# Moving the split of x ahead of the softmax's two stages, and the low parts of N to one engine

## The chip, the cores and the metric

The kernel runs on one core of a Trainium2 chip. The metric is the device time of one execution in microseconds (us). A core has TensorE (PE in the profile, its weight loads PEld), VectorE (DVE), ScalarE (ACT), GpSimd (POOL) and SyncE (SP), which here only issues DMAs. Each engine works through its own instructions in order; semaphores join them.

## The reference

Sixteen batches of 1024 rows of width 512. Each row of x attends to the 64 context rows of its batch with 16 heads of width 64, the result is added to x, and a chain of three 512x512 matrices with a tanh is added to that. Cut to its core:

```python
def xattn(x, latents, shift, scale, ...):      # x: context (64 rows a batch), latents: layernorm(x), 1024 rows
    xn = layernorm(x, ln1_w, ln1_b); ln = layernorm(latents, ln2_w, ln2_b)
    q = ln @ Wq; k, v = split(xn @ Wkv)
    q = q * (1 + scale) + shift                # by batch and head
    attn = softmax(einsum('bihd,bjhd->bhij', q, k) / 8)
    return einsum('bhij,bjhd->bihd', attn, v) @ Wout
x = x + xattn(ctx_1024, layernorm(x), fside, fside, ...)
x = x + tanh(layernorm(x) @ weight @ aux_weight1 @ aux_weight2 + bias)
```

## The kernel before, in words

The work is folded so that a tile of 128 rows needs few matmuls. For each batch, Wq and k are multiplied ahead into one matrix M (512 x 1024: 16 heads times 64 context rows), v and Wout into one matrix N (1024 x 512), and the three feed-forward matrices into W3. Every fp32 operand of a matmul is split in two fp32r parts, a high one (a cast on ScalarE, written `..._hi`) and a low one (the rest, by a subtraction on VectorE or GpSimd, `..._lo`), and a product is three passes: high by high, high by low, low by high (`passes`, line 162; line 168 issues the passes that need the high part of the tile, line 173 those that need its low part).

There are T = 128 tiles, 8 to a batch. `run` calls one function for each engine and slot t (`slot_pe`, `slot_act`, `slot_dve`, `slot_pool`, `slot_sp`), and the order of the calls in each function is the order of that engine's queue, written out by hand. It is a pipeline over slots. In slot t:

- PE makes the scores of tile t in two halves q = 0 and 1 of 512 columns (24 matmuls, from `xT_hi` and `xT_lo`, which are single buffers), then the output product of tile t-2 in two halves (24 matmuls, from `pT_hi`, `pT_lo` and N), then the feed-forward product of tile t-4 (12 matmuls). Between them stand matmuls for the M and N of later batches: four short ones (lines 937 to 940) up to slot 89, and four (lines 756, 757) in the slots that make N.
- DVE: turning and low part of the second half of p of tile t-2, then for each half the scale and bias of the scores (line 1399) and the row maximum (1404), then for each half the sum (1410) and its reciprocal (1413), then the addition of the output to x (1511), then the turning (1421) and low part (1430) of the first half of p of tile t-1.
- POOL: the last addition of tile t-5 (1571), then the subtraction of the maximum (1547) for both halves, with the low part of a landed piece of M between them (1021), then the two normalisations (1554), then `xT_lo` of tile t+1 (1085) and two small powers (1070, 1559).
- ACT: `pT_hi` of the second half (1296), the tanh (1337), the statistics of the second layernorm, `x2T_hi`, the high part of a piece of M (1017), the first exponential (1291), the statistics of the first layernorm of tile t+1 (1052 to 1059), the second exponential, `xT_hi` of tile t+1 (1080), evacuations, and `pT_hi` of the first half of tile t-1.
- SP issues all DMAs in one queue: the turned x of tile t+1 at the slot's start (`load_xT`, line 639, which waits for `xT_lo` of tile t), x of tile t+2, four reads of p that turn it between partitions (1145), four of x2 (1157), the result (1166), pieces of M, and, behind the normalisations, the two writes of p (1127).

From batch 4 on N is made in pairs of batches. In each of the 8 slots t = 8(b-1)+2+p PE makes two banks for the head pair p of batches b and b+1 (`n2_pe`), ACT evacuates bank 0 and DVE bank 1 (`n2_evacuate`, two copies of 64 partitions each, lines 765 and 766) to a raw buffer. The split into `N_hi` (`n2_hi`, line 775, ACT) and `N_lo` (`n2_lo`, line 781) of the even batch comes in one go at the **border slot** t = 33, 49, 65, 81, 97 and 113 (`border(t)`: the second slot of an even batch from 4 on), since the buffers come free only there: eight pieces. ACT makes pieces 0 to 3, then `pT_hi`, then 4 to 7. DVE makes the low parts of pieces 0 and 1 ahead of `pT_lo`, and of 2, 3 and 7 behind it; POOL makes 4, 5 and 6. The odd batch has one piece a slot, on DVE. PE waits for the low parts through `n2_made` in the slot after.

```python
BY_POOL = (4, 5, 6)
border = lambda t: t % TPB == 1 and t // TPB in range(STACKED, B, 2)
def xT_split_hi(act, u):            # also waits for the scores of tile u - 1: xT_hi is a single buffer
    act.wait_ge(s_xT, 16 * u if u else 16)
    at_least(act, s_sc[1], u)
```

## Time and profile before

| what | value |
|---|---|
| median of 3 runs | 2071.06 us (2065.18 to 2071.54) |
| profiled execution, its own time | 2069.4 us |
| its span | 2067.6 us |
| granted TensorE clock, mean over the span | 0.997 |
| PE, PEld busy | 2017.8 us (98%), 1661.6 us (80%) |
| DVE, ACT, POOL busy | 1573.8 us (76%), 1364.1 us (66%), 1393.7 us (67%) |
| DMA packets' time, share of 16 engines, queue of SP | 79.2% |

The profile is one execution. The span runs from its first instruction to its last, 1.8 us short of the execution's own time. Matmuls are pipelined: in a full PE one of 512 columns starts every 0.227 us and each is shown as 0.39 us long, so the idle time ahead of a matmul in the rows is less than what its start is late. In the chain of work that ended last PE has 32%, DVE 18%, SP's queue 15%, ACT 10%.

### The profile page before, as it was taken

What the parts mean: (1) busy time and instruction counts of PE and PEld (TensorE: products, weight loads), DVE (VectorE), ACT (ScalarE), POOL (GpSimd) and SP (SyncE); (2) the same over time, 40 slices, a digit from 0 to 9 for tenths busy, and PEclk for the clock granted to TensorE, in tenths of its full rate; (3) what the DMA queues carried; (4) which work ended last, traced back from release to release, by engine and by line L of the source; (5) the groups of instructions that cost most, each with busy time, mean ns of one, the idle gap of its engine ahead of it and who ended that gap; (6) DMA issues with size and microseconds to landing.
All of it is one profiled execution on the core that took longest, in us unless ns stands there. A gap on an engine that the chain in (4) does not pass through costs nothing.

```text
span 2067.6 us, 31929 instructions
## 1 busy us (share of the span) xinstructions
PE 2017.8 (98%) x9072; PEld 1661.6 (80%) x9072; DVE 1573.8 (76%) x2470; ACT 1364.1 (66%) x3125; POOL 1393.7 (67%) x1529
## 2 busy tenths in 40 slices
PE   8998999999999999999999999999999999999998
PEld 6887878888788788878888788878888788878887
DVE  7567876776677787787777877778777877888776
ACT  4455667666676766776667676666666666666654
POOL 2136767666577777677766777777776777777664
PEclk9999999999999999999999999999999999999999
DMA  7657989989788788978898798888877567866663
GB/s 259 196 176 219 275 233 256 265 241 262 210 249 256 207 236 242 260 217 225 233 260 242 205 234 238 243 229 221 230 228 241 171 204 208 236 197 196 189 171 121
DMA packets 524864, 464.11 MB, mean 224 GB/s; under 512 B 56720, under 2 KB 416272, under 8 KB 524688
## 3 DMA queue, kind: packets, MB, share of 16 engines
q1 hardware_dynamic: 524688, 462.06, 79.2%
q8 instruction: 74, 1.21, 0.3%
q14 instruction: 102, 0.84, 0.1%
HBM read 279.64 MB, written 182.26 MB: 223 GB/s over the span
## 4 chain that ended last, share of the span: by engine, by line
PE 32%; DVE 18%; SPq 15%; ACT 10%; issue 10%; POOL 7%; DMA 4%; DVEq 0%; ACTq 0%; POOLq 0%
PE bank L168 12%; PE bank L1246 8%; PE bank L173 6%; POOL area L1547 5%; PE bank L1251 4%; DVE pT_lo L1430 3%; ACT area L1291 3%; DVE turned L1421 3%; DVE area L1399 2%; ACT pT_hi L1296 2%; DVE row_max L1404 2%; SPq L1127 2%; SPq L726 2%; SPq L1145 2%; SPq L1157 2%
## 5 line engine op out<-in xcount | busy, mean ns | idle before, releaser
L1547 POOL TENSOR_TENSOR area<-area,row_max 128x256 f32<-128x256 f32 x512 | 353.0, 710 | 105.3 <-DVE row_max L1404 100.1
L1296 ACT CAST pT_hi<-turned 128x512 fp32r<-128x512 f32 x256 | 159.3, 622 | 400.8 <-DVE turned L1421 400.7
L168 PE MATMUL bank<-M_hi,xT_hi 128*128 128x512 f32 x1024 | 402.7, 393 | 14.4 <-ACT xT_hi L1080 14.4
L168 PE MATMUL bank<-M_lo,xT_hi 128*128 128x512 f32 x1024 | 401.4, 392 | 0.0
L1571 POOL TENSOR_TENSOR area<-area 128x512 f32<-128x512 f32 x127 | 165.4, 1302 | 269.1 <-ACT area L1337 269.1
L1554 POOL TENSOR_TENSOR area<-area,row_inv 128x512 f32<-128x512 f32 x256 | 269.1, 1051 | 113.7 <-DVE row_inv L1413 113.7
L1410 DVE TENSOR_REDUCE row_sum<-area 128x8 f32<-128x512 f32 x256 | 174.5, 682 | 169.5 <-ACT area L1291 168.6
L1430 DVE TENSOR_TENSOR pT_lo<-turned,pT_hi 128x512 fp32r<-128x512 f32 x256 | 196.6, 768 | 112.3 <-ACT pT_hi L1296 103.7
L173 PE MATMUL bank<-M_hi,xT_lo 128*128 128x512 f32 x1024 | 276.0, 391 | 3.6 <-POOL xT_lo L1085 3.6
L1246 PE MATMUL bank<-N_hi,pT_hi 128*128 128x512 f32 x640 | 249.5, 390 | 3.2 <-ACT pT_hi L1296 1.8
L1246 PE MATMUL bank<-N_lo,pT_hi 128*128 128x512 f32 x640 | 249.6, 390 | 1.5 <-issue 1.4
L168 PEld LDWEIGHTS bank<-M_hi,xT_hi 128*128 128x128 f32 x1024 | 193.8, 189 | 57.5 <-ACT xT_hi L1080 17.3
L1291 ACT ACTIVATE area<-area 128x512 f32<-128x512 f32 x256 | 160.4, 626 | 115.6 <-POOL area L1547 115.5
L173 PEld LDWEIGHTS bank<-M_hi,xT_lo 128*128 128x128 f32 x1024 | 190.9, 188 | 48.6 <-POOL xT_lo L1085 9.8
L168 PEld LDWEIGHTS bank<-M_lo,xT_hi 128*128 128x128 f32 x1024 | 194.0, 189 | 39.8
L168 PE MATMUL bank<-W_hi,x2T_hi 128*128 128x512 f32 (+1 forms) x512 | 199.1, 389 | 1.1 <-ACT x2T_hi L1317 1.1
L168 PE MATMUL bank<-W_lo,x2T_hi 128*128 128x512 f32 (+1 forms) x512 | 199.1, 389 | 0.0
L1399 DVE SCALAR_TENSOR_TENSOR area<-bank,rs,area 128x512 f32<-128x512 f32 x256 | 185.6, 725 | 3.4 <-DMA m_scratch<-area 3.4
L1421 DVE STREAM_TRANSPOSE turned<-p_moved 128x512 f32<-128x512 f32 x256 | 180.5, 705 | 5.3 <-DMA p_moved<-p_scratch 1.4
L1404 DVE TENSOR_REDUCE row_max<-area 128x8 f32<-128x512 f32 x256 | 175.7, 686 | 8.8
L1056 ACT ACTIVATE bank<-area,st 128x512 f32<-128x512 f32 x254 | 175.9, 693 | 8.3
L1450 DVE TENSOR_TENSOR x2T_lo<-turned,x2T_hi 128x512 fp32r<-128x512 f32 x126 | 109.3, 868 | 86.6 <-ACT x2T_hi L1317 85.4
(211 smaller groups left out, 4547.9 us busy)
## 6 DMA issues: line engine op xcount, KB each, us to landing
p_scratch<-area SPq DMA_DIRECT2D x256, 256.0 KB, 3.1
p_moved<-p_scratch SPq DMA_DIRECT2D x512, 128.0 KB, 4.2
area<-x_dram SPq DMA_DIRECT2D x128, 256.0 KB, 5.0
area<-x_turned_dram SPq DMA_DIRECT2D x128, 256.0 KB, 4.4
x_scratch<-area SPq DMA_DIRECT2D x127, 256.0 KB, 3.4
x_moved<-x_scratch SPq DMA_DIRECT2D x508, 64.0 KB, 3.5
y_dram<-area SPq DMA_DIRECT2D x127, 256.0 KB, 3.5
land<-m_scratch SPq DMA_DIRECT2D x120, 256.0 KB, 3.2
```

Source lines behind the costliest of these rows:

```text
L168: mm = eng.matmul(ps, sh, mv, start=(n == 0), stop=False)
L173: mm = eng.matmul(ps, sl, mh, start=False, stop=(k == len(pairs) - 1))
L1056: act.activation(junk_ps[:], src, ACT.Square, bias=st[:, 1:2], accum_out=st[:, 2:3]).then_inc(s_sq, 1)
L1246: mm = pe.matmul(O_ps[:], st(pT_hi, k), n_cols(mv, k), start=(k == 0 and mv is hi), stop=False)
L1291: act.activation(s, s, ACT.Exp).then_inc(s_ex[q], 1)
L1296: act.copy(half_of(pT_hi, q), turned[:]).then_inc(s_pTh[q], 1)
L1399: dve.scalar_tensor_tensor(out=half_of(S[t % 2], q), in0=S_ps[q][:], scalar=rs1[:, 0:1], in1=half_of(bias, q), op0=ALU.mult, op1=ALU.add). ...
L1404: dve.tensor_reduce(row_max[t % 2][:, q * H2:(q + 1) * H2], heads(half_of(S[t % 2], q)), AX_XY, ALU.max).then_inc(s_mx[q], 1)
L1421: dve.transpose(turned[:].rearrange("p (k g r) -> p k g r", k=4, g=4), blocks).then_inc(done, 1)
L1430: dve.tensor_tensor(half_of(pT_lo, q), turned[:], half_of(pT_hi, q).bitcast(F32), ALU.subtract).then_inc(s_pTl[q], 1)
L1547: last = pool.tensor_tensor(s, s, row.to_broadcast([P, 2, 4, J2]), ALU.subtract)
L1554: pool.tensor_tensor(s, s, inv, ALU.mult).then_inc(s_p[q], 1)
```

## The change

In every slot t from 3 on, ACT makes `xT_hi` of tile t+1 ahead of the first exponential instead of behind the second, and POOL makes `xT_lo` of tile t+1 ahead of the two normalisations instead of behind them. At the border slots DVE makes all eight low parts, in two groups of 2 and 6, and ACT evacuates both banks. The counters of the semaphores follow.

```diff
--- before.py
+++ after.py
@@ -603,7 +603,7 @@
         s_n, s_nh, s_nl = sem("s_n"), sem("s_nh"), sem("s_nl")
         s_bin = sem("s_bin")
         s_x2a, s_x2n = sem("s_x2a"), sem("s_x2n")
-        s_last, s_nfree, s_nl_pool = sem("s_last"), sem("s_nfree"), sem("s_nl_pool")
+        s_last, s_nfree = sem("s_last"), sem("s_nfree")
         s_yl, s_bnl, s_rsl = sem("s_yl"), sem("s_bnl"), sem("s_rsl")
         s_kh, s_kl = sem("s_kh"), sem("s_kl")
         s_wo2, s_nev = sem("s_wo2"), sem("s_nev")
@@ -696,9 +696,6 @@
             used, free = free[1], (used, free[0])
         N_of = lambda b: [n_bufs[i] for i in n_at[b]]
         stage_of = lambda b, c: n_raw[:, (n_at[b][1] * PAIRS + c) * D:(n_at[b][1] * PAIRS + c + 1) * D]
-        BY_POOL = (4, 5, 6)
-        BY_DVE = {0: [c for c in range(PAIRS) if c not in BY_POOL], 1: list(range(PAIRS))}
-        lo_before = lambda b: PAIRS * min(b, STACKED) + sum(len(BY_DVE[a % 2]) for a in range(STACKED, b))
         split_at = {TPB * b + c - TPB + 2: (b, c) for b in range(STACKED + 1, B, 2) for c in range(PAIRS)}
         border = lambda t: t % TPB == 1 and t // TPB in range(STACKED, B, 2)
         n2_ps = banks[2:4]
@@ -778,14 +775,7 @@
             for c in cs:
                 eng.wait_ge(s_nh, PAIRS * b + c + 1)
                 hi, lo = (n_cols(y, c) for y in N_of(b))
-                eng.tensor_tensor(lo, stage_of(b, c), hi.bitcast(F32),
-                                  ALU.subtract).then_inc(s_nl if c in BY_DVE[b % 2] else s_nl_pool, 1)
-
-        def n2_made(pe, b, q):
-            of_half = range(4 * q, 4 * q + 4)
-            pe.wait_ge(s_nl, lo_before(b) + sum(c < 4 * q + 4 for c in BY_DVE[b % 2]))
-            if b % 2 == 0 and any(c in BY_POOL for c in of_half):
-                pe.wait_ge(s_nl_pool, len(BY_POOL) * ((b - STACKED) // 2) + sum(c < 4 * q + 4 for c in BY_POOL))
+                eng.tensor_tensor(lo, stage_of(b, c), hi.bitcast(F32), ALU.subtract).then_inc(s_nl, 1)
 
         m_where = lambda c: ((c // 2) % 4, 2 * (c // 8) + c % 2)
         in_pairs = lambda a: a.rearrange("p (i a j) -> p i a j", i=2, j=J2)
@@ -1234,10 +1224,8 @@
                 at_least(pe, s_x2, u)
             for q in range(2):
                 if tile_of(t - 2):
-                    if m == 2 and u < TPB * STACKED:
+                    if m == 2:
                         pe.wait_ge(s_nl, u + 4 + 4 * q)
-                    elif m == 2:
-                        n2_made(pe, u // TPB, q)
                     hi, lo = N_of(u // TPB)
                     ks = range(4 * q, 4 * q + 4)
                     pe.wait_ge(s_pTh[q], u + 1)
@@ -1349,6 +1337,8 @@
                 xT_split_hi(act, t + 1)
             if t > 2:
                 evacuate("A")
+                if t < T - 1:
+                    xT_split_hi(act, t + 1)
             if t < T:
                 exp(0)
             if t < 2:
@@ -1365,12 +1355,13 @@
                 fold_n_act(act, 0, range(5, 6))
                 land_hi(act, 0)
                 fold_n_act(act, 0, range(6, 7))
-            elif t < T - 1:
+            elif t == 2:
                 xT_split_hi(act, t + 1)
-            if t == 2:
                 ln1_stats(act, 3, 3)
             if t in stacked_at:
                 n2_evacuate(act, act.copy, *stacked_at[t], 0)
+                if border(t):
+                    n2_evacuate(act, act.copy, *stacked_at[t], 1)
             evacuate("C")
             if border(t):
                 n2_hi(act, t // TPB, range(0, 4))
@@ -1511,7 +1502,8 @@
                 dve.tensor_tensor(xr[u % RING], O_ps[:], xr[u % RING], ALU.add).then_inc(s_x2, 1)
             sum_tile("C")
             if t in stacked_at:
-                n2_evacuate(dve, dve.tensor_copy, *stacked_at[t], 1)
+                if not border(t):
+                    n2_evacuate(dve, dve.tensor_copy, *stacked_at[t], 1)
             if tile_of(t - 1):
                 if t >= 4:
                     dve.wait_ge(s_x2Tl, t - 3)
@@ -1523,13 +1515,13 @@
                     maximum(0, 2)
                 turn_p(0, t - 1)
                 if border(t):
-                    n2_lo(dve, t // TPB, BY_DVE[0][0:2])
+                    n2_lo(dve, t // TPB, range(0, 2))
                 if t == 1:
                     read_scores(1, 2)
                     maximum(1, 2)
                 pT_lo_part(0, t - 1)
             if border(t):
-                n2_lo(dve, t // TPB, BY_DVE[0][2:])
+                n2_lo(dve, t // TPB, range(2, 8))
             if t in split_at:
                 b, c = split_at[t]
                 n2_lo(dve, b, [c])
@@ -1590,19 +1582,17 @@
             if t == 2:
                 land_lo(pool, 1)
                 xT_split_lo(pool, 3)
+            if 2 < t < T - 1:
+                xT_split_lo(pool, t + 1)
             if t < T:
                 normalise(0)
                 normalise(1)
             if t == 1:
                 land_lo(pool, 0)
-            if 2 < t < T - 1:
-                xT_split_lo(pool, t + 1)
             if 1 < t < T - 1:
                 pow1(pool, t + 1)
             if tile_of(t - 4) and t - 4 < LAST - 1:
                 pow2(t - 4)
-            if border(t):
-                n2_lo(pool, t // TPB, BY_POOL)
             if t == 5:
                 land_lo(pool, t)
```

The border slot t = 33 on ACT. In this listing an instruction's line is that of its own file; `Wo_hi<-n_raw,N_lo` and `N_lo<-n_raw` name the buffers that hold N at that batch. Before:

```order
L1017 CAST M_hi<-land 128x512
L1291 ACTIVATE area<-area 128x512
L1052 ACTIVATE bank,st<-area 128x512
L1054 ACTIVATE st<-st 128x1
L1056 ACTIVATE bank,st<-area,st 128x512
L1059 ACTIVATE var<-st,eps 128x1
L1291 ACTIVATE area<-area 128x512
L1080 CAST xT_hi<-area 128x512
L765 COPY n_raw<-bank 64x512
L766 COPY n_raw<-bank 64x512
L968 COPY evac<-bank 128x2x4x64
L775 CAST N_lo<-n_raw 128x512 x4
```

and now:

```order
L1007 CAST M_hi<-land 128x512
L1070 CAST xT_hi<-area 128x512
L1279 ACTIVATE area<-area 128x512
L1042 ACTIVATE bank,st<-area 128x512
L1044 ACTIVATE st<-st 128x1
L1046 ACTIVATE bank,st<-area,st 128x512
L1049 ACTIVATE var<-st,eps 128x1
L1279 ACTIVATE area<-area 128x512
L762 COPY n_raw<-bank 64x512
L763 COPY n_raw<-bank 64x512
L762 COPY n_raw<-bank 64x512
L763 COPY n_raw<-bank 64x512
```

The cast of `xT_hi` stands ahead of the first exponential (the first ACTIVATE of area), and a second pair of copies has come in ahead of the casts of N.

The same slot on POOL, before:

```order
L1021 TENSOR_TENSOR M_lo<-land,M_hi 128x512
L1547 TENSOR_TENSOR area<-area,row_max 128x256 x2
L1554 TENSOR_TENSOR area<-area,row_inv 128x512 x2
L1085 TENSOR_TENSOR xT_lo<-area,xT_hi 128x512
L1070 TENSOR_TENSOR rs<-var,minus_half 128x1
L1559 TENSOR_TENSOR rs<-var,minus_half 128x1
L781 TENSOR_TENSOR Wo_hi<-n_raw,N_lo 128x512 x3
```

and now:

```order
L1011 TENSOR_TENSOR M_lo<-land,M_hi 128x512
L1539 TENSOR_TENSOR area<-area,row_max 128x256 x2
L1075 TENSOR_TENSOR xT_lo<-area,xT_hi 128x512
L1546 TENSOR_TENSOR area<-area,row_inv 128x512 x2
L1060 TENSOR_TENSOR rs<-var,minus_half 128x1
L1551 TENSOR_TENSOR rs<-var,minus_half 128x1
```

`xT_lo` has gone ahead of the normalisations (two instructions on row_inv), which it does in the other slots too, and the three low parts of N are gone. On DVE, behind the addition to x, before:

```order
L1511 TENSOR_TENSOR area<-bank,area 128x512
L765 COPY n_raw<-bank 64x512
L766 COPY n_raw<-bank 64x512
L1421 STREAM_TRANSPOSE turned<-p_moved 128x512
L781 TENSOR_TENSOR Wo_hi<-n_raw,N_lo 128x512 x2
L1430 TENSOR_TENSOR pT_lo<-turned,pT_hi 128x512
L781 TENSOR_TENSOR Wo_hi<-n_raw,N_lo 128x512 x3
```

and now:

```order
L1502 TENSOR_TENSOR area<-bank,area 128x512
L1412 STREAM_TRANSPOSE turned<-p_moved 128x512
L778 TENSOR_TENSOR Wo_hi<-n_raw,N_lo 128x512 x2
L1421 TENSOR_TENSOR pT_lo<-turned,pT_hi 128x512
L778 TENSOR_TENSOR Wo_hi<-n_raw,N_lo 128x512 x6
```

The two copies have left DVE, and the last group of low parts has grown from three to six.

## Rows read from the trace of the kernel before

**Rows 1.** The page, part 1: busy time, share of the span, instructions
```profile
PE 2017.8 (98%) x9072; PEld 1661.6 (80%) x9072; DVE 1573.8 (76%) x2470; ACT 1364.1 (66%) x3125; POOL 1393.7 (67%) x1529
```

**Rows 2.** Waits of PE: waiter and its line <- whom it waited for, us in total, times, longest
```profile
PE bank L168 <- ACT xT_hi L1080: 14.4, 7, 2.5
...
PE bank L173 <- POOL xT_lo L1085: 3.6, 6, 0.8
```

**Rows 3.** Timeline, PE: start us, us long; first matmuls of slots 34, 35, 36, 38
```profile
664.52 0.39 PE L168 MATMUL bank<-M_hi,xT_hi 128*128 128x512 f32 x1
...
681.83 0.79 PE L168 MATMUL bank<-M_hi,xT_hi 128*128 128x512 f32 x1 [2.09 <-ACT xT_hi L1080]
...
697.62 0.39 PE L168 MATMUL bank<-M_hi,xT_hi 128*128 128x512 f32 x1
...
725.82 0.39 PE L168 MATMUL bank<-M_hi,xT_hi 128*128 128x512 f32 x1
```

**Rows 4.** Timeline, slot 34: POOL's first normalisation and xT_lo; ACT's xT_hi
```profile
680.42 1.05 POOL L1554 TENSOR_TENSOR area<-area,row_inv 128x512 f32<-128x512 f32 x1
...
683.36 1.29 POOL L1085 TENSOR_TENSOR xT_lo<-area,xT_hi 128x512 fp32r<-128x512 f32 x1
...
681.17 0.60 ACT L1080 CAST xT_hi<-area 128x512 fp32r<-128x512 f32 x1
```

**Rows 5.** Timeline, border slot 33: low parts of N on DVE and on POOL
```profile
666.87 5.18 DVE L781 TENSOR_TENSOR Wo_hi<-n_raw,N_lo 128x512 fp32r<-128x512 f32 x3
...
666.76 4.74 POOL L781 TENSOR_TENSOR Wo_hi<-n_raw,N_lo 128x512 fp32r<-128x512 f32 x3 [0.83 <-ACT N_lo L775]
```

**Rows 6.** Lines 781, 765, 1430: duration ns min/median/max, first and last start us
```profile
L781 DVE TENSOR_TENSOR Wo_lo<-n_raw,N_hi x16: 679/680/686, 685.1 to 1495.3; 128x512 fp32r<-128x512 f32 x16
...
L765 ACT COPY n_raw<-bank x48: 572/577/583, 558.2 to 1839.7; 64x512 f32<-64x512 f32 x48
...
L1430 DVE TENSOR_TENSOR pT_lo<-turned,pT_hi x256: 681/693/1025, 174.3 to 2049.7; 128x512 fp32r<-128x512 f32 x128
```

**Rows 7.** Line 639, the load of the turned x: all 128; that of slot 65
```profile
DMA to landing us min/median/max: 2.9/4.4/6.8
...
area<-x_turned_dram SPq DMA_DIRECT2D x1, 256.0 KB, 5.7
```

**Rows 8.** Timeline, SP: that load's issue in border slots 33, 65, 81, 97
```profile
655.06 0.84 SPq L639 DMA_DIRECT2D area<-x_turned_dram  x1
...
1129.06 0.71 SPq L639 DMA_DIRECT2D area<-x_turned_dram  x1
...
1369.05 0.75 SPq L639 DMA_DIRECT2D area<-x_turned_dram  x1
...
1597.87 0.47 SPq L639 DMA_DIRECT2D area<-x_turned_dram  x1
```

**Rows 9.** Timeline, ACT: the first exponential of the same slots
```profile
658.17 0.63 ACT L1291 ACTIVATE area<-area 128x512 f32<-128x512 f32 x1 [0.82 <-POOL area L1547]
...
1131.88 0.63 ACT L1291 ACTIVATE area<-area 128x512 f32<-128x512 f32 x1 [0.71 <-POOL area L1547]
...
1371.86 0.63 ACT L1291 ACTIVATE area<-area 128x512 f32<-128x512 f32 x1 [0.71 <-POOL area L1547]
...
1604.38 0.64 ACT L1291 ACTIVATE area<-area 128x512 f32<-128x512 f32 x1 [0.82 <-POOL area L1547]
```

**Rows 10.** Timeline, DVE: the scores' scaling, first half, in slots 100 and 101
```profile
1648.83 0.71 DVE L1399 SCALAR_TENSOR_TENSOR area<-bank,rs,area 128x512 f32<-128x512 f32 x1
...
1662.60 0.71 DVE L1399 SCALAR_TENSOR_TENSOR area<-bank,rs,area 128x512 f32<-128x512 f32 x1
```

**Rows 11.** Timeline, slot 103: pT_lo on DVE beside xT_lo on POOL
```profile
1685.71 0.96 DVE L1430 TENSOR_TENSOR pT_lo<-turned,pT_hi 128x512 fp32r<-128x512 f32 x1 [0.81 <-ACT pT_hi L1296]
...
1684.82 1.30 POOL L1085 TENSOR_TENSOR xT_lo<-area,xT_hi 128x512 fp32r<-128x512 f32 x1
```

**Rows 12.** Timeline, slot 33: POOL's second normalisation
```profile
662.44 1.05 POOL L1554 TENSOR_TENSOR area<-area,row_inv 128x512 f32<-128x512 f32 x1 [0.89 <-DVE row_inv L1413]
```

## The prediction

> **What bounds the kernel now.** I read the page's busy shares first. PE has 98% [rows 1], so nearly all of the span is matmul work that this change leaves alone; what can be gained is the time in which PE stands still. The table of PE's waits comes next: of the waits on another engine in the tile loop the largest is for `xT_hi` of the next tile, 14.4 us in 7 waits, with 3.6 us for `xT_lo` behind it [rows 2]. So I looked for the place. The starts of the slots' first matmuls give it [rows 3]: slots 36 and 37 together take 725.82 - 697.62 = 28.20 us, 14.10 each, and slots 34 and 35, with the same matmuls, take 697.62 - 664.52 = 33.10. So 4.9 us are lost behind the border slot 33, and 2.09 of them show as PE idle until ACT has cast `xT_hi` [rows 3]. A border comes six times; with one such wait from the last unstacked fold these are the 7 waits. All borders together are worth about 6 x 4.9 = 29 us.
>
> Why is ACT late there? Because the ring of the softmax is: ACT, DVE and POOL hand a tile round (scaling, maximum, subtraction, exponential, sum, normalisation, turning, split), and a border adds eight casts and eight low parts. In ordinary slots the ring needs 13.77 us: that is the distance of the first scaling of slot 100 to that of slot 101 [rows 10], while PE's own work there is 60 matmuls, at the 0.227 us of a full PE 13.6 us (the 14.10 of [rows 3] has four short ones more). Up to slot 97 PE has slots of 14.1 us and more, so the ring catches up between borders. Behind slot 97 it hardly can.
>
> **Part 1: `xT_lo` and `xT_hi` go forward.** `xT_lo` starts at 683.36 in slot 34, and the first normalisation, whose place it takes, at 680.42: it comes 2.94 us earlier [rows 4]. Its own 1.29 us now stand ahead of both normalisations. The second waits for its sums anyway, idle for 0.89 us in slot 33 [rows 12], so I charge it 1.3 - 0.9 = 0.4 us, the first 1.3; the two writes of p on SP's queue stand behind them, with the second write's followers (x2's write, loads of weights, the next turned x). Cover: p is read a slot later. `xT_hi`'s 0.60 us [rows 4] go into ACT's idle 0.82 or 0.71 us ahead of the first exponential, where it waits for POOL [rows 9]: no cost if x has landed, and 0.6 us less behind the second exponential. PE's wait is then for `xT_lo`, so I take 2.94 us a border.
>
> **Part 2: the border's low parts.** Three of them on DVE take 5.18 us while POOL's three take 4.74 in the same microseconds [rows 5]; on DVE alone one is 0.68 [rows 6]. So the two engines hold each other up, 1.73 us each instead of 0.68. Now DVE's group is six: 6 x 0.68 = 4.1 instead of 5.18, 1.1 us less. The Trainium skill, SBUF — State Buffer, section Who interferes with whom, has DVE instructions with two SBUF inputs and GpSimd's reads exclude each other for a whole instruction; these rows agree. A price without that rule, DVE at its present 1.73 for each of six, would be 10.4 us and a border 5.2 us longer. Against the 1.1 stands the second evacuation: two copies at 0.58 [rows 6] on ACT ahead of the casts of N, less the `xT_hi` that left, 1.16 - 0.60 = 0.6 us later. Bounds 0.5 and 1.1; I take **0.8 us**, since DVE in turn loses its own two copies ahead of the first low part.
>
> **Part 3: the added wait.** ACT's queue now stops ahead of the first exponential until the turned x has landed, and everything of the softmax stands behind it. The load is issued in the same slot, by SP, at the tail of its queue, and lands 2.9 to 6.8 us later, 4.4 in the median [rows 7]. With 0.7 us for the cast and its start, the exponential can begin, against its start now [rows 8, 9]:
> slot 33: 655.06 + 4.4 + 0.7 = 660.2, 2.0 us later than 658.17;
> slot 49: taken as 1.0, between slot 33's 2.0 and slot 97's nothing;
> slot 65: landing 5.7 here [rows 7], 1129.06 + 6.4 = 1135.5, 3.6 us later than 1131.88;
> slot 81: 1369.05 + 5.1 = 1374.2, 2.3 us later than 1371.86;
> slot 97: 1597.87 + 5.1 = 1603.0, ahead of 1604.38: nothing. Slot 113 I take as slot 97.
> This delay goes round the ring into the border and comes off the gain.
>
> **The sum.** A stall can be given back once, since the ring is caught up before the next border:
> border 33: 2.94 + 0.8 - 2.0 = 1.7;
> border 49: 2.94 + 0.8 - 1.0 = 2.7;
> border 65: 2.94 + 0.8 - 3.6 = 0.1;
> border 81: 2.94 + 0.8 - 2.3 = 1.4.
> Behind slot 97 the ring sets the end (13.77 against 13.6), and there the 2.94 only let PE run ahead of work it must wait for at the end. What counts is what the ring itself loses: 2 x 0.8 = 1.6 us, and in the slots where `xT_lo` on POOL overlaps `pT_lo` on DVE 0.96 [rows 11] - 0.69 [rows 6] = 0.27 us, in about 20 slots 5.4 us, since the new place has only reductions of one input beside it. Of these 7.0 I take 5.0, as PE's own 13.6 caps the ring at 0.17 a slot wherever no stall is left to give back. Sum 1.7 + 2.7 + 0.1 + 1.4 + 5.0 = **10.9 us**. The profiled execution had 2069.4 us, 1.7 under the median of the runs; 2069.4 - 10.9 = 2058.5, and I forecast **2058.5 us** as the median.
>
> **The rivals.**
> *A: every border stall goes.* The load lands in time because SP's queue, too, follows the ring, and PE finds no second thing late. 29 us less: **2040 us**. Against it: rows 8 and 9, and that `pT_hi` of the first half is the next thing PE needs, with slack of the same size as the gain. Chance 0.10.
> *B: nothing moves.* The late load of part 3 takes back what part 1 gives, in the last stretch too (0 to 4 us gained): **2068 us**. For it: in slot 65 it does so to 0.1 us, and SP's queue gets its writes of p 0.4 to 1.3 us later, which makes the load later still. PE's 98% speak for it in a general way. The Trainium skill, Perfetto Trace Analysis, section Identifying the Most-Contended Engine, has one speed up the engine with the highest occupancy and not judge TensorE by its matmul busy time; PE's matmuls lose nothing here, so by the first half of that rule the gain is nil, and rows 3 show where the busy share hides 4.9 us. Chance 0.25.
> *C: slower.* The wait closes a ring that was open: load of the turned x, `xT_hi`, exponentials, second normalisation, second write of p, and behind it on SP the next such load. Worked out: landing 4.4, cast and start 0.7, start of the first exponential to end of the second normalisation 662.44 + 1.05 - 658.17 = 5.3 [rows 9, 12] plus the 0.4 of part 1, write to next load 2.6 (an estimate: four issues of 0.5 to 0.8 as in [rows 8]), together 13.4 us. It decides once the landing averages over 4.6 us in slots where PE has 13.6 (over 5.1 where it has 14.1). At a mean landing of 5.2 us, still well inside 2.9 to 6.8, it is 14.2 us: 0.6 over in some 22 slots, 0.1 over in some 24, +15.6 us, less the 5.9 that borders 33 to 81 give: 2069.4 + 9.7, **2079 us**. Against it: the median of 4.4. Chance 0.10.
> My forecast has the remaining 0.55.
>
> **How the numbers follow.** About 0.3%, 6.2 us, is what a measurement of this kernel can tell from no change. Faster by more than that: nearly all of the forecast, whose lower end (0.5 a border at part 2, 2 us for the last stretch) is a gain of 5.9 - 1.2 + 2 = 6.7, and A; where the loads are later than I put them it falls under 6.2, so 0.62. Within 0.3%: B and that part, 0.28. Slower: C, 0.10. The range: A's 2040 and C's 2079 are left out with 0.2 between them; from the forecast with the last stretch at its full 7.0 us, the load never late (+8.9, of which border 49 can't use all) and part 2 at 1.1 a border, I get a gain of about 21, 2048; B's upper end with the median's own scatter is 2070. So 2048 to 2070.
>
> **What would show it.** In the profile after, PE's wait for ACT `xT_hi` should be almost gone behind the borders, with PE waiting for `xT_lo` or `pT` instead. The low parts of N on DVE should last 0.68 us each and none be on POOL. ACT should show idle time ahead of `xT_hi` whose releaser is the DMA from the turned x, longest around slot 65. `pT_lo` should be at 0.69 in all ordinary slots. Slots 34 and 35 should take about 1.7 us less than 33.1. I am wrong if ACT does not wait for the load at the borders (then A), or if the first scalings in slots 100 to 106 are not nearer than 13.77 us (then B), or farther (then C).

## The result

The changed kernel takes 2079.49 us (median of 5 runs, 2077.00 to 2083.62), the kernel before in the same comparison 2068.09 (5 runs, 2065.18 to 2071.54): ratio 1.0055, interval 1.0035 to 1.0075. It is slower by more than the 0.3% that can be told from no change. The prediction was 2058.5 us and faster. The profiled execution of the changed kernel had 2077.0 us, a span of 2075.2.

Part 1 of the page of the changed kernel (compare [rows 1]), then three rows of the kernel before and of the changed kernel each, from the view that cuts the span into stretches. The stretches end at the first scores matmul of slots 10, 26 and 36 and at the span's end. Columns: stretch, its length, busy us of each engine with the number of instructions, mean granted clock of TensorE, share of the DMA engines, GB/s.

```profile
PE 2017.7 (97%) x9072; PEld 1664.3 (80%) x9072; DVE 1539.9 (74%) x2476; ACT 1365.6 (66%) x3137; POOL 1323.8 (64%) x1511
```
Kernel before:
```profile
292.09:540.23 248.14, 245.93 (x1139) 203.81 (x1138) 176.88 (x278) 168.38 (x381) 168.15 (x184) 1.00 0.90 244
540.23:697.62 157.39, 151.85 (x675) 124.01 (x673) 117.74 (x183) 107.27 (x248) 109.87 (x122) 0.99 0.83 238
697.62:2067.60 1369.98, 1347.76 (x6009) 1110.63 (x6007) 1067.35 (x1651) 917.77 (x2132) 986.10 (x1081) 1.00 0.78 218
```
Changed kernel:
```profile
293.39:559.35 265.96, 249.42 (x1138) 204.95 (x1137) 170.60 (x278) 165.30 (x381) 161.73 (x184) 0.99 0.83 228
559.35:719.24 159.89, 152.20 (x674) 123.80 (x673) 114.60 (x181) 107.91 (x249) 102.81 (x118) 0.99 0.82 232
719.24:2075.20 1355.96, 1342.87 (x6009) 1110.89 (x6007) 1043.43 (x1660) 921.48 (x2142) 931.29 (x1067) 1.00 0.80 221
```

The last stretch gained 14.0 us, and for it the prediction had 9.2. Slots 26 to 36, with the first border, lost 2.5 where 1.7 were to be gained. Slots 10 to 26, of which the prediction does not speak, lost 17.8 us: more than the whole loss of the span, 7.6 (the first 10 slots and the set-up are 1.3 us longer, the rest of that difference). DVE, ACT and POOL are less busy there than before, and PE's 3.5 us more come with a clock of 0.99 instead of 1.00; nobody has more work in these slots, somebody waits. Each stretch is one execution, and that of the changed kernel was 2.5 us under its median. From slot 26 on the run "split early from slot 26" below has the changed kernel's code, and its profile has 4.7 us more there (1520.6 against 1515.9). So the 17.8 us stand clear of such scatter, the 2.5 do not by themselves. The table of waits says who waits (changed kernel; waiter and line <- whom it waited for, us in total, times, longest):

```profile
ACT evac L958 <- DMA m_scratch<-evac: 51.2, 18, 4.3
ACT xT_hi L1070 <- DMA area<-x_turned_dram: 34.4, 33, 2.7
PE bank L929 <- ACT evac L958: 11.5, 8, 1.7
PE bank L1234 <- ACT pT_hi L1284: 8.1, 6, 1.9
PE bank L753 <- issue: 6.5, 6, 2.1
PE bank L173 <- POOL xT_lo L1075: 1.0, 4, 0.4
```
PE's wait for `xT_hi` [rows 2] has left the table, as forecast. In its place PE waits for an evacuation at line 958, and ACT waits there for a DMA. The same wait in the kernel before:
```profile
ACT evac L968 <- DMA m_scratch<-evac: 24.7, 17, 4.1
```

**The ring that was not seen.** In slots 10 to 25 PE makes two short tiles a slot for the M of later batches, at two places in its queue that the code calls C and D. Both leave through one buffer, `evac` (`evacuate` and `store` in the slot functions). ACT copies C into it behind the second exponential; SP stores it, behind the second write of p, the write of x2 and a load; when the store has landed, ACT copies D, near the head of its queue for the next slot, and the exponentials stand behind that. That closes a ring: each of these steps waits for the one before, once round in every slot. One round in the kernel before (ACT, then SP; start us, length, engine and line, what, idle time before it and what ended that):

```profile
354.82 0.59 ACT L968 COPY evac<-bank 128x512 f32<-128x512 f32 x1 [1.33 <-DMA m_scratch<-evac]
...
361.36 0.63 ACT L1291 ACTIVATE area<-area 128x512 f32<-128x512 f32 x1 [0.32 <-POOL area L1547]
...
362.40 0.58 ACT L968 COPY evac<-bank 128x512 f32<-128x512 f32 x1
...
369.92 0.59 ACT L968 COPY evac<-bank 128x512 f32<-128x512 f32 x1 [1.53 <-DMA m_scratch<-evac]
...
364.15 0.54 SPq L1127 DMA_DIRECT2D p_scratch<-area  x1
...
366.44 0.63 SPq L978 DMA_DIRECT2D m_scratch<-evac  x1
```
and in the changed kernel, same slot:
```profile
361.32 0.59 ACT L958 COPY evac<-bank 128x512 f32<-128x512 f32 x1 [3.96 <-DMA m_scratch<-evac]
...
367.95 0.61 ACT L1279 ACTIVATE area<-area 128x512 f32<-128x512 f32 x1
368.47 0.56 ACT L958 COPY evac<-bank 128x512 f32<-128x512 f32 x1
...
377.35 0.59 ACT L958 COPY evac<-bank 128x512 f32<-128x512 f32 x1 [3.04 <-DMA m_scratch<-evac]
...
370.07 0.55 SPq L1117 DMA_DIRECT2D p_scratch<-area  x1
370.67 0.64 SPq L711 DMA_DIRECT2D wo_scratch<-Wo_hi  x1
371.36 0.61 SPq L1117 DMA_DIRECT2D p_scratch<-area  x1
...
373.85 0.61 SPq L968 DMA_DIRECT2D m_scratch<-evac  x1
```

| step of the round | before | changed |
|---|---|---|
| copy of D to second exponential | 6.54 | 6.63 |
| to SP's issue of the second write of p | 2.79 | 3.41 |
| to the issue of the store of C | 2.29 | 2.49 |
| to ACT's next copy of D (landing and start) | 3.48 | 3.50 |
| round | 15.10 | 16.03 |

PE's own work there is 14.60 us a slot (29.20 for two in most pairs of the kernel before). A round of 15.1 is already longer, but it falls behind slowly and has PE's slack to use up; at 16.0 the slack is gone after two slots: slots 12 to 15 together took 58.4 us before and 63.2 now. POOL shows where the largest part, 0.62 us, is from: `xT_lo` stands ahead of both normalisations (before, then changed).
```profile
363.07 1.05 POOL L1554 TENSOR_TENSOR area<-area,row_inv 128x512 f32<-128x512 f32 x1 [0.74 <-DVE row_inv L1413]
```
```profile
367.78 1.26 POOL L1075 TENSOR_TENSOR xT_lo<-area,xT_hi 128x512 fp32r<-128x512 f32 x1
369.00 2.06 POOL L1546 TENSOR_TENSOR area<-area,row_inv 128x512 f32<-128x512 f32 x2
```
The second normalisation ends at 371.06, 3.11 us behind the start of the second exponential, where the kernel before has 361.36 to 363.07 + 1.05 = 364.12, 2.76. That is the 0.35 more that the prediction charged as 0.4. The other 0.27 are SP's own issues: the first write of p, now late with the first normalisation, and a store of shares of Wout (line 711) are still being issued when the second normalisation ends, so the second write goes out 0.30 us behind that end, where it was 0.03 before. What the prediction did not ask is who waits for the write. The Trainium skill, Perfetto Trace Analysis, section Optimization Strategy, has it that the same gap repeating over a stretch, on the engine that should be saturated, can mean too few buffers. The rows agree: that engine is PE, its wait for the evacuation (line 929) comes 8 times, and behind it ACT's wait for the one `evac` 18 times.

### The profile page after: what moved, and what is told of

Read it like the earlier page. It is cut to its first block, busy times and chain, and to the rows that moved or that the text cites. A ratio compares the mean times of both kernels' runs of the same rounds, so it can differ in the third digit from the quotient of the medians.

```text
span 2075.2 us, 31929 instructions
## 1 busy us (share of the span) xinstructions
PE 2017.7 (97%) x9072; PEld 1664.3 (80%) x9072; DVE 1539.9 (74%) x2476; ACT 1365.6 (66%) x3137; POOL 1323.8 (64%) x1511
## 4 chain that ended last, share of the span: by engine, by line
PE 25%; DVE 18%; SPq 16%; ACT 13%; issue 10%; POOL 10%; DMA 7%; DVEq 0%; ACTq 0%; POOLq 0%
PE bank L168 10%; POOL area L1539 6%; PE bank L1234 6%; PE bank L173 5%; DVE pT_lo L1421 3%; DVE turned L1412 3%; SPq L1117 3%; ACT area L1279 3%; PE bank L1239 3%; ACT pT_hi L1284 3%; DMA area<-x_turned_dram 3%; DMA m_scratch<-evac 3%; ACT bank L1042 2%; DVE area L1390 2%; DVE row_max L1395 2%
## 5 line engine op out<-in xcount | busy, mean ns | idle before, releaser
L1284 ACT CAST pT_hi<-turned 128x512 fp32r<-128x512 f32 x256 | 159.0, 621 | 434.8 <-DVE turned L1412 434.8
L1546 POOL TENSOR_TENSOR area<-area,row_inv 128x512 f32<-128x512 f32 x256 | 264.4, 1050 | 19.1 <-DVE row_inv L1404 19.0
L1421 DVE TENSOR_TENSOR pT_lo<-turned,pT_hi 128x512 fp32r<-128x512 f32 x256 | 177.8, 695 | 122.2 <-ACT pT_hi L1284 120.9
L1279 ACT ACTIVATE area<-area 128x512 f32<-128x512 f32 x256 | 159.9, 624 | 44.9 <-POOL area L1539 44.4
L1011 POOL TENSOR_TENSOR M_lo<-land,M_hi 128x512 fp32r<-128x512 f32 x120 | 155.5, 1296 | 50.1 <-ACT M_hi L1007 50.1
```

The costliest lines, as they stand in the source:

```text
L1279: act.activation(s, s, ACT.Exp).then_inc(s_ex[q], 1)
L1284: act.copy(half_of(pT_hi, q), turned[:]).then_inc(s_pTh[q], 1)
L1421: dve.tensor_tensor(half_of(pT_lo, q), turned[:], half_of(pT_hi, q).bitcast(F32), ALU.subtract).then_inc(s_pTl[q], 1)
L1546: pool.tensor_tensor(s, s, inv, ALU.mult).then_inc(s_p[q], 1)
```

## The experiments

All were timed beside the kernel before, whose median lay between 2067.85 and 2069.81 us; the ratio is to the kernel before of the same comparison. "10-26", "26-36", "36-end" are the stretches of the tables above; "borders" is the sum of the six stretches 33-36, 49-52, 65-68, 81-84, 97-100, 113-116. These three columns come from one profiled execution each. Four kernels have the same code at the borders but for the place of one store (changed, split early from slot 26, store of C first, store of C behind write 1), and their sums run from 273.6 to 276.1: a difference of 2 us between two of these sums says nothing.

| kernel | median us | ratio to before, interval | 10-26 | 26-36 | borders |
|---|---|---|---|---|---|
| before | 2068.09 | | 248.1 | 157.4 | 284.7 |
| changed | 2079.49 | 1.0055 (1.0035 to 1.0075) | 266.0 | 159.9 | 273.6 |
| split early from slot 26 | 2063.09 | 0.9972 (0.9961 to 0.9983) | 248.6 | 159.2 | 274.6 |
| low part late again | 2080.83 | 1.0062 (1.0046 to 1.0078) | 247.9 | 162.6 | 294.9 |
| store of C first | 2057.26 | 0.9941 (0.9926 to 0.9955) | 244.5 | 156.6 | 276.1 |
| border's part alone | 2070.71 | 1.0010 (1.0000 to 1.0020) | 247.8 | 158.4 | 284.1 |
| load ahead of write 0 | 2114.43 | 1.0220 (1.0204 to 1.0236) | 267.1 | 162.4 | 267.1 |
| the same, store of C first | 2117.12 | 1.0240 (1.0217 to 1.0262) | 245.5 | 168.9 | 272.6 |
| before, store of C first | 2068.26 | 0.9990 (0.9976 to 1.0003) | 244.5 | 159.0 | 285.1 |
| splits of x alone | 2083.85 | 1.0071 (1.0056 to 1.0085) | 267.3 | 156.4 | 278.9 |
| load behind write 0 | 2082.57 | 1.0061 (1.0042 to 1.0080) | 275.3 | 154.3 | 268.2 |
| the same, store of C first | 2078.01 | 1.0039 (1.0025 to 1.0054) | 248.6 | 160.0 | 271.1 |
| evacuations alone | 2084.71 | 1.0069 (1.0051 to 1.0088) | 267.4 | 159.8 | 280.7 |
| store of C behind write 1 | 2058.46 | 0.9956 (0.9942 to 0.9970) | 246.9 | 159.1 | 275.5 |

**The ring, taken out of the change.** The changed kernel with both splits of x at their old places in slots 3 to 25:
```diff
             if t > 2:
                 evacuate("A")
-                if t < T - 1:
+                if 26 <= t < T - 1:
                     xT_split_hi(act, t + 1)
...
-            elif t == 2:
+            elif t < 26:
                 xT_split_hi(act, t + 1)
...
-            if 2 < t < T - 1:
+            if 26 <= t < T - 1:
                 xT_split_lo(pool, t + 1)
             if t < T:
                 normalise(0)
                 normalise(1)
+            if 2 < t < 26:
+                xT_split_lo(pool, t + 1)
```


> The changed kernel with both splits of x at their old places in slots 3 to 25 and at the new ones from slot 26 on; the border part stays. Theory R (store ring): in slots 10 to 25, where two short tiles of M a slot go through the one buffer evac, the second write of p is 0.6 us later behind xT_lo, so evac's store behind it on SP is too, ACT waits for it ahead of both exponentials, and the ring store, landing, evacuation, exponentials, normalisations, write, store takes 16.0 us a slot against PE's 14.6. Then slots 10 to 26 fall back from 266 to 248 us, the rest stays as in the changed kernel, and the whole is 18 us under it, about 2060, 6 to 9 under the kernel before. Theory L (load wait): the loss is the wait of ACT for the turned x, 34.4 us in 33 waits, most of them behind slot 26; then this run gains little against the changed kernel, at most 5 us.

It took 2063.09 us, 16.4 less than the changed kernel (18 were expected), and 10-26 is back at 248.6: more than the whole loss against the kernel before was in these slots, and what remains of the change is a gain. The rival, that ACT's wait for the turned x is the loss, would have given at most 5 us.

**Which of the two splits.** The changed kernel with `xT_lo` alone back behind the normalisations, in all slots:
```diff
-            if 2 < t < T - 1:
-                xT_split_lo(pool, t + 1)
             if t < T:
                 normalise(0)
                 normalise(1)
+            if 2 < t < T - 1:
+                xT_split_lo(pool, t + 1)
```


> The changed kernel with xT_lo behind the normalisations again; xT_hi stays ahead of the first exponential, and the border part stays. Theory R: the write of p is on time again, so slots 10 to 26 take 248 to 252 us instead of 266 (xT_hi is still in the ring, 0.5 us less 0.3 of a wait that it fills), while PE waits for xT_lo behind the borders again: 2065 to 2071. Theory H (rival: it is xT_hi's 0.6 us on ACT ahead of the exponentials that stretches the ring): slots 10 to 26 stay at 260 or more and the whole is 2080 or more. Theory L: as H in the total, with ACT's wait for the turned x still over 30 us.

The stretch 10-26 is cured (247.9 us) with `xT_hi` early and ACT's wait for the load as long as before, so it is `xT_lo`, not `xT_hi` or its wait. The total, 2080.83, is 10 us over the expected range and as high as the rival had it, but for another reason: elsewhere the late low part costs more than had been gained, the borders sum to 294.9. ACT's wait for the load, and PE's at the borders:
```profile
ACT xT_hi L1070 <- DMA area<-x_turned_dram: 33.3, 32, 3.3
...
PE bank L173 <- POOL xT_lo L1075: 27.1, 11, 3.3
```

**The ring, shortened at another place.** The changed kernel, SP's store moved ahead of the second write of p:
```diff
             next_wst("B")
             store("B")
+            if t >= 10:
+                store("C")
             if t < T:
                 write_p(1)
...
             next_wst("C")
-            store("C")
+            if t < 10:
+                store("C")
```


> The changed kernel with one DMA of SP's queue moved: from slot 10 on the store of the tile at place C stands ahead of the second write of p instead of behind the write of x2. Theory R: the store is issued about 2.5 to 4 us earlier, the ring of slots 10 to 25 opens, ACT's wait for the store of evac (51.2 us) falls under 10, slots 10 to 26 take at most 250 us, and the whole is about 2057 to 2062. Theory L: the store is beside the point, less than 3 us change.

2057.26 us, 22.2 less than the changed kernel and 11 less than the kernel before. PE is busy in all of 10-26 now. ACT's copies of D in slots 14 and 15 come 14.73 us apart instead of 16.03, and the wait for the store ahead of them, 3.96 and 3.04 us in the changed kernel, is nothing and 0.60:
```profile
294.04:538.52 244.48, 244.48 (x1139) 204.45 (x1138) 178.73 (x278) 168.06 (x381) 166.90 (x184) 1.00 0.87 247
```
```profile
354.27 0.56 ACT L958 COPY evac<-bank 128x512 f32<-128x512 f32 x1
...
369.00 0.59 ACT L958 COPY evac<-bank 128x512 f32<-128x512 f32 x1 [0.60 <-DMA m_scratch<-evac]
```

**The border's part alone**, on the kernel before: eight low parts on DVE, both evacuations on ACT, splits of x unmoved.
```diff
-        BY_POOL = (4, 5, 6)
+        BY_POOL = ()
...
             if t in stacked_at:
                 n2_evacuate(act, act.copy, *stacked_at[t], 0)
+                if border(t):
+                    n2_evacuate(act, act.copy, *stacked_at[t], 1)
...
-            if t in stacked_at:
+            if t in stacked_at and not border(t):
                 n2_evacuate(dve, dve.tensor_copy, *stacked_at[t], 1)
...
-            if border(t):
-                n2_lo(pool, t // TPB, BY_POOL)
```


> The kernel before with the border part alone: all low parts of N on VectorE, both banks of the border's pair evacuated by ScalarE. By the prediction's part 2 it is worth 0.8 us a border, at most 4.8 us in all, 2064 to 2068; slots 10 to 26 stay as in the kernel before. If the two engines did not hold each other up, a low part would stay at 1.77 us on VectorE and a border would be 5 us longer, 2095 or so.

Nothing gained: 2070.71 us. The low parts did get short; over all borders DVE is busy for 34.4 us with 48 of them where it had 38.6 with 30. Of the three groups of 16 the slowest:
```profile
L781 DVE TENSOR_TENSOR Wo_hi<-n_raw,N_lo 128x512 fp32r<-128x512 f32 x16 | 12.2, 821 | 2.7 <-ACT N_lo L775 2.7
```
But ACT, not DVE, is what PE waits for: its wait for `xT_hi` stays, and the one for `pT_hi`, 1.8 us in 2 waits before, has grown. The second evacuation on ACT is the likely reason; no run has the low parts moved without it in this kernel.
```profile
PE bank L168 <- ACT xT_hi L1080: 14.6, 7, 2.4
...
PE bank L1246 <- ACT pT_hi L1296: 5.1, 7, 1.5
```

**The load one slot earlier.** The changed kernel, to take ACT's wait for turned x away; `load_xT(sp, t + 2)` ahead of the first write of p:
```diff
-            if 1 < t < T - 1:
+            if t == 2:
                 load_xT(sp, t + 1)
...
+            if 1 < t < T - 2:
+                load_xT(sp, t + 2)
             if t < T:
                 write_p(0)
```


> The changed kernel, but SP issues the load of turned x one slot earlier: that of tile t+2 in slot t ahead of the first write of p, in place of that of tile t+1 at the slot's start. This takes away ScalarE's wait for that load ahead of the first exponential (34.4 us in 33 waits in the changed kernel). Ring theory (the single evac buffer's store and evacuation set the period of slots 10 to 26): this stretch stays at 262 to 268 us, since the run with the late low part had the same load wait and 247.9 us there; what goes is the wait ahead of the exponentials at the borders (slots 33, 49, 65, 81, 97, 113), 0 to 1.5 us each, so 2070 to 2079 us, and ScalarE's wait for turned x under 5 us. Load theory (the wait for turned x is what made the changed kernel slow): the stretch falls to 255 us or less and the total below 2068.

The wait went and 10-26 stayed at 267.1, as the ring theory had it, but its total was missed by 35 us. I had costed an issue and overlooked the wait in it: `load_xT` waits for `xT_lo` of the tile before, since the landing buffer is single, and SP, with all its transfers behind, stood there. PE gets it as a wait for the shares of Wout, which the changed kernel does not have:
```profile
SPq L639 <- POOL xT_lo L1075: 138.5, 63, 4.2
```
```profile
PE bank L753 <- DMA wo<-wo_scratch: 31.3, 21, 3.1
```
The 138.5 us are not all new standstill, since SP's wait ahead of the writes of p fell from 271.4 to 82.3 us; what counts is which transfers stand behind the stop. The Trainium skill, DMA: Bandwidth & Descriptors, section Anatomy of one DMA — SWDGE (gpsimd) path, says that a semaphore wait is spent by the sequencer that issues, ahead of the transfer; that section is on GpSimd's path, and the row agrees for SP. With the store of C moved too:

> The changed kernel with SP's store of the short tile of place C ahead of the second write of p (from slot 10 on) and with the load of turned x a slot earlier. Ring theory: slots 10 to 26 stay at the 244.5 us of the run with the store moved alone, and the earlier load gives what it gives in the run with the load alone, so 2051 to 2058 us against 2057.3 with the store alone. Load theory: both together give no more than the better of the two alone plus 1 us in slots 10 to 26, and the borders gain over 1 us each, so 2045 to 2052.

2117.12 us, 59 us or more over both expectations, so this kernel decided nothing but the stretch 10-26, 245.5 us, again the ring's.

**The store first, without the change**, on the kernel before (same edit as above):

> The kernel before with SP's store of the short tile of place C ahead of the second write of p from slot 10 on, nothing else. Ring theory: in the kernel before the ring takes 15.1 us a slot against 14.6 of TensorE and its lag is mostly hidden, so the move gives only what was left over in slots 16 to 26 (36.33 and 36.23 us where 34.6 were had with the store moved, and 29.57 for 29.20): 3.0 to 3.7 us, stretch 10 to 26 at 244 to 246 us and the total at 2064 to 2066. Rival (the gain of 22 us over the changed kernel came from a better order on SP for every slot, not from the ring that the change had tightened): it gives 10 us or more here too, 2058 or less.

Stretch 10-26 at 244.5, as expected, 3.7 us less; the total, 2068.26 against 2069.81 in this comparison, is level with before (1.6 us less, with an interval from 0.6 more to 5.0 less), and 2064 to 2066 was missed; in the profiles 1.6 of the 3.7 are given back in slots 26 to 36. The rival's 10 us are excluded: the 22 us that the same edit gave the changed kernel were the ring that the change had tightened.

**Part 1 alone**, the splits of x early in the kernel before, the border as it was:

> The kernel before with the first part of the change alone: x's high part ahead of the first exponential and its low part ahead of the normalisations in every slot; the border's low parts and evacuations stay as before (three of eight low parts on GpSimd, the pair's second half on VectorE). Ring theory: slots 10 to 26 hold no border, so they take 264 to 268 us as in the changed kernel; since the border's part alone was worth nothing (2070.7 against 2068.3), the total is 2077 to 2081. Rival (the border's part gives its gain only once x is split early, or costs something then): the border stretches 33 to 36, 49 to 52, 65 to 68, 81 to 84, 97 to 100, 113 to 116 differ from the changed kernel's by over 1 us each, and the total is 2083 or more, or 2074 or less.

Stretch 10-26 is the ring's, 267.3. The total missed the 2077 to 2081 and lies over the rival's 2083, by ratio to before at 2082.8, so at its edge. The test by single stretches decides nothing: five of the six differ from the changed kernel's by over 1 us in one direction or the other, but so do five of six in the run split early from slot 26, which has the changed kernel's code there. What the sums allow is this: 278.9 here and 280.7 in the run "evacuations alone" below, against 273.6 to 276.1 in the four kernels with the low parts on DVE. The means are 4.9 us apart, 0.8 a border. In the medians the same gain is 3.3 us, which is not clear of noise. Alone, on the kernel before, the part was worth nothing.

**The load behind the first write of p**, where SP has no wait of its own for it:
```diff
             if t < T:
                 write_p(0)
+            if 1 < t < T - 2:
+                load_xT(sp, t + 2)
```


> The changed kernel with the load of turned x a slot earlier, this time behind the first write of p (which waits for the first normalisation, and this stands behind xT_lo on GpSimd, so the load brings SP no wait of its own; ahead of that write it made SP wait 138.5 us for xT_lo in 63 rounds). Ring theory: slots 10 to 26 stay at 262 to 268 us; ScalarE's wait for turned x goes, the borders gain up to 1.5 us each and the slots between them stay at 189.65: 2068 to 2079 us. Load theory (what the early high part costs is its wait for the load): stretch at 255 us or less and total below 2068. Third, if a load ahead of the shares of the second stage is itself what costs: slots 36 to 49 and 52 to 65 again over 192 us, total over 2085.

The load theory fell: 10-26 went *up* to 275.3. The ring theory's 262 to 268 and its total were missed too, since the load, 0.63 us of SP's time, now stands ahead of the ring's store: the same round in slot 14 takes 16.71 us, and PE's wait for the evacuation grew. Elsewhere the move gave back what part 3 of the prediction had charged for the late load: 26-36 at 154.3 against 159.9, and the borders 5.4 us shorter.
```profile
PE bank L929 <- ACT evac L958: 16.5, 11, 1.7
```
With the store of C first:

> The changed kernel with SP's store of place C ahead of the second write of p and the load of turned x a slot earlier behind the first write of p. Ring theory: slots 10 to 26 at 244.5 us as with the store alone, the borders as in the run with this load alone; 2048 to 2057 us, against 2057.3 with the store alone. If the load's place costs more than its wait: over 2060.

2078.01, worse than the store alone by 20.8 us. The gain was missed, and the other branch of the expectation (over 2060) came true. The ring is nearly cured (248.6), but slots 36 to 49 and 52 to 65 take 194.2 and 195.2 us instead of 189.65; PE waits in their last slots and right behind (45 to 49, 63 and 64) for the shares of Wout. Why that wait is there in this kernel and not in the one with the load alone (189.65 in both stretches) was not settled.
```profile
PE bank L753 <- DMA wo<-wo_scratch: 18.3, 16, 2.3
```

**The evacuations alone**: as part 1 alone, and the pair's second half evacuated by ACT at the border; low parts still shared with POOL.
```diff
                 n2_evacuate(act, act.copy, *stacked_at[t], 0)
+                if border(t):
+                    n2_evacuate(act, act.copy, *stacked_at[t], 1)
...
-            if t in stacked_at:
+            if t in stacked_at and not border(t):
                 n2_evacuate(dve, dve.tensor_copy, *stacked_at[t], 1)
```


> The changed kernel with the low parts of the border shared with GpSimd again (three of eight), the pair's second half still evacuated by ScalarE. With both parts at the border the six stretches 33 to 36, 49 to 52, ... 113 to 116 sum to 273.6 us, without them to 278.9. If the shared low parts were the cost, as the prediction's second part had it (1.77 us each on VectorE beside GpSimd's, 0.68 alone), the sum here is 277 to 281 and the total 2082 to 2085 us, as without the border's part. If it is ScalarE's evacuation that gains, the sum is 273 to 275 and the total 2078 to 2080.

Borders 280.7, total 2084.71, both as expected: the gain is the low parts', as the prediction's part 2 had it. What the evacuations cost (1.8 us in the sums, 280.7 less 278.9) is within the scatter.

**The store behind the second write of p**, ahead of x2's write and the load:
```diff
             if t < T:
                 write_p(1)
+            if t >= 10:
+                store("C")
```


> The changed kernel with SP's store of place C right behind the second write of p from slot 10 on, ahead of x2's write and the wst load that stood between them. In the changed kernel one round of the evac ring takes 16.02 us in slot 14 (6.63 from the evacuation of D to the second exponential, 3.40 to the issue of the second write of p, 2.49 to the issue of the store, 3.43 to its landing, 0.07 to the next evacuation), TensorE's slot 14.60. Ring theory: some 1.8 of the 2.49 us go, the round is 14.2 us and hides under TensorE, slots 10 to 26 take 244.5 to 249 us, the total is 2056 to 2064. Rival (the store must not stand behind a wait for GpSimd's normalisations at all: the ring's part that xT_lo has lengthened is the wait in the second write of p): the stretch stays above 255 us and the total above 2068.

2058.46 us and 246.9 in 10-26, as expected. In slot 14 the store is issued 0.66 us behind the second write of p, where it was 2.49. So the wait behind the normalisations may stay in the ring; taking 1.8 us out at another place of it, on SP, does nearly as much.

## Why the prediction was wrong

- **The failed step** is in part 1: "Cover: p is read a slot later." It let the late second write of p, and what stands behind it on SP, cost nothing. It named those followers (x2's write, loads of weights, the next turned x) but not the store of `evac`, the one with a consumer that was already waiting, 24.7 us in the table of waits of the kernel before. Nor did it look at slots 10 to 26 at all. The 0.4 us on the second normalisation was right to 0.05; with the queue's additions it became 0.9 us a round, over a ring 0.5 us longer than PE's slot, and cost 17.8 us. Three runs show it from three sides: 16.4 us come back with both splits at their old places there, the stretch is at 247.9 with `xT_lo` alone moved back, and 22.2 us come back with the store moved.
- **A wait gone behind the borders: right.** PE's wait for `xT_hi` is gone. For `xT_lo` and `pT_hi`, where the prediction expected PE to wait instead, it waits 1.0 and 8.1 us. Slots 34 and 35 took 32.1 us, 1.0 less than 33.1 where 1.7 were forecast (timeline of PE, first matmuls of slots 34 and 36, as [rows 3]):
```profile
687.11 0.39 PE L168 MATMUL bank<-M_hi,xT_hi 128*128 128x512 f32 x1
...
719.24 0.39 PE L168 MATMUL bank<-M_hi,xT_hi 128*128 128x512 f32 x1
```
  With the load's wait taken away too (load behind write 0), the six borders are 284.7 - 268.2 = 16.5 us shorter than before, 2.8 each, of the 2.94 + 0.8 that parts 1 and 2 had put there.
- **Part 2: about right in size, and conditional.** 0.8 a border forecast, some 0.8 in the profiles with x split early; nothing alone. A low part now lasts 0.68 us in the median, as forecast, but in four of the six borders the seventh still takes 1.78, beside a subtraction of two inputs on POOL (`k_parts`, line 899). The sum added the parts as if independent; they are not. That ACT's chain hides DVE's gain until `xT_hi` has left it fits PE's waits in the run with the border's part alone.
- **Part 3: right mechanism, wrong place.** ACT idles for the load, but at the border slots for only 0.02, 0.05, 0.90, 0.00, 0.00 and 0.00 us, where 2.0, 1.0, 3.6, 2.3 were forecast; the 33 waits lie in the slots ahead of them:
```profile
649.66 0.62 ACT L1070 CAST xT_hi<-area 128x512 fp32r<-128x512 f32 x1 [2.11 <-DMA area<-x_turned_dram]
...
666.94 0.62 ACT L1070 CAST xT_hi<-area 128x512 fp32r<-128x512 f32 x1 [2.23 <-DMA area<-x_turned_dram]
```
  So the exponentials are late in the slots ahead, and by the order of the queues that delay reaches slot 33, where PE waits for POOL's `v_lo`, a stop that the kernel before does not have:
```profile
679.35 0.73 POOL L743 TENSOR_TENSOR v_lo<-v_raw,v_hi 128x256 fp32r<-128x256 f32 x1
...
680.18 0.47 PE L753 MATMUL bank<-wo,v_hi 128*128 128x512 f32 x1 [1.11 <-issue]
```
  Slots 29, 32 and 33 took 15.01 us each before and 16.09, 16.09 and 16.36 in the changed kernel; with the load behind write 0 they are at 15.01 again. These 3.5 us are why the stretch with the first border lost 2.5 instead of gaining 1.7. From slot 26 to the end the kernel with the load behind write 0 takes 1510.0 us and the changed one 1515.9, so the late load costs about 6, known only to some 5; part 3 had 8.9 for it.
- **The last stretch: more than forecast, for another reason.** The scalings of slots 100 and 101 are 13.49 us apart, where [rows 10] have 13.77:
```profile
1663.99 0.71 DVE L1390 SCALAR_TENSOR_TENSOR area<-bank,rs,area 128x512 f32<-128x512 f32 x1
...
1677.48 0.71 DVE L1390 SCALAR_TENSOR_TENSOR area<-bank,rs,area 128x512 f32<-128x512 f32 x1
```
  As forecast, no `pT_lo` behind slot 97 is over 0.8 us long any more, where 20 were at 0.95 or more. But PE's slots stop at its own 13.60, so the ordinary slots (100 to 105 and 116 to 125) gave only 2.2 us of the 5.0 taken: before, some of them were at 13.6 already. From slot 84 to the end the profile gave 9.0 us; 7.3 of them are the borders 97 and 113, 3.8 and 3.4, whose stall the prediction took for already paid by the ring. It was not: PE's slots behind them are at 13.60, so the ring no longer sets the end.
- **Rival C** had the result's size, 2079 us, by a ring through SP's queue; that the number fits is chance. The ring that closed was another: `evac`'s, not the turned x's, in slots 10 to 26, not behind slot 97. With 0.10 on slower, all rings of SP's queue together had been given too little.

The forecast for what the change does behind slot 26 was 10.9 us. With the early split from slot 26 on it was 5.2 us (2068.3 in its comparison, less 2063.1). With the store of C first in both kernels it was 10: the ratios to before are 0.9941 and 0.9990, 0.0049 of 2068. Which of the two is nearer is open, since the moved store also stands elsewhere in the slots behind 26.

## What to carry to other kernels

An instruction that is put ahead of what a write on a DMA queue waits for delays that write and every later transfer of that queue; before the delay is costed at nothing, each follower needs its own answer to two questions: is its buffer single, and does the table of waits already show somebody waiting for it. Do this in every stage of the program, also in those where nothing is to be gained: a ring that is just hidden (15.1 us against 14.6) shows as no stall of TensorE and still has no room. And where two chains take turns as the last, parts of a change do not add: measure one alone and the other without it.

## What the runs showed beside that

- A stall of about 2 us can cost twice. After 1.88 us of idle PE was granted 0.53 of its clock in the changed kernel (stretch 698.20 to 700.40, matmuls 0.43 us apart instead of 0.227), which is about the lower of its two levels, 1.2 GHz; with the store moved, after the same 1.88 us in the same place, it stayed at full clock (2.4 GHz), with matmuls 0.23 us apart. No run shows why it fell in one and not in the other:
```profile
697.53 0.47 PE L1234 MATMUL bank<-N_lo,pT_hi 128*128 128x512 f32 x1 [1.88 <-ACT pT_hi L1284]
```
```profile
698.20:700.40 2.20, 2.20 (x7) 1.70 (x6) 2.03 (x3) 2.10 (x7) 1.13 (x1) 0.53 0.82 234
```
```profile
674.47 0.47 PE L1237 MATMUL bank<-N_lo,pT_hi 128*128 128x512 f32 x1 [1.88 <-ACT pT_hi L1287]
674.77 0.40 PE L1237 MATMUL bank<-Wo_hi,pT_hi 128*128 128x512 f32 x1
675.01 0.39 PE L1237 MATMUL bank<-N_lo,pT_hi 128*128 128x512 f32 x1
```
  That is one reason why the border stretches of one profile scatter by a microsecond or two each, and a sum of six says more than any one of them.
- Moving a transfer of unchanged size on SP's queue moved the time of the changed kernel by +35 us (load ahead of write 0, which brought a wait with it) or -22 us (store of C first). The order of this queue, whose DMA engines are busy 79% of the time, was the strongest lever of all that were tried.
